# A graph layer on one core: branches taken earlier, the last four steps in another order, and DVE's picks and bf16 parts as tensor_tensor

## The reference, cut to what matters

```python
h = maximum(layernorm(x), 0)                      # x: 6250 nodes x 64
p1 = tanh(h @ pp_W1 + pp_b1) @ pp_W2 + pp_b2
inter = concatenate([p1[src], p1[dst]], -1)       # 200000 edges, dst sorted
inter = ((inter @ pi_W1 + pi_b1) @ pi_W2 + pi_b2) @ pi_W3
inter = inter.reshape(E, 64, 8)
i1 = einsum('ecb,eb->ec', inter, edge_attr)       # 8 numbers for each edge
i1 = tanh(i1 @ ii_W1 + ii_b1) @ ii_W2 + ii_b2
out = x + segment_sum(i1, dst, 6250)
```

## Time and profile before

| | |
|---|---|
| time, median of 3 runs | 2033.84 us (2032.79 to 2038.43) |
| profiled execution: its own time | 2041.94 us |
| its span | 2039.9 us |
| PE busy | 1756.2 us (86%) |
| POOL busy | 1506.6 us (74%) |
| DVE busy | 1325.6 us (65%) |
| ACT busy | 1099.3 us (54%) |
| mean granted TensorE clock | 0.939 |

### The profile page before, as it was taken

One profiled execution on the slowest core, in us unless ns is written; L12 is line 12 of the kernel. 1 busy time (PEld: TensorE's weight loads), 2 busy tenths in 40 slices (PEclk: granted clock), 3 DMA queues, 4 the chain that ended last, 5 costly groups with the idle time before them and its releaser, 6 DMA issues.

```text
span 2039.9 us, 54797 instructions
## 1 busy us (share of the span) xinstructions
PE 1756.2 (86%) x19956; PEld 1145.7 (56%) x19956; DVE 1325.6 (65%) x1894; ACT 1099.3 (54%) x2401; POOL 1506.6 (74%) x1582
## 2 busy tenths in 40 slices
PE   5698888888889888888888988989888888888988
PEld 4465555555555555555555555555555555555765
DVE  6676666666666666666666666666666666666665
ACT  4565555555555555555555555555555555555554
POOL 2777777777777777777777777777777777777774
PEclk9799999999999999999999999899999998998999
DMA  5533233222332332322323323323233233222231
GB/s 124 132 68 62 54 62 61 56 60 55 60 61 55 61 62 55 63 58 58 60 55 60 61 55 62 60 55 61 55 61 60 55 60 61 55 57 55 58 73 40
DMA packets 261682, 126.82 MB, mean 62 GB/s; under 512 B 183545, under 2 KB 233704, under 8 KB 261432
## 3 DMA queue, kind: packets, MB, share of 16 engines
q1 hardware_dynamic: 210915, 74.15, 17.1%
q0 software_dynamic: 50048, 51.35, 12.8%
q10 hardware_dynamic: 594, 0.10, 0.0%
HBM read 119.47 MB, written 6.00 MB: 62 GB/s over the span
## 4 chain that ended last, share of the span: by engine, by line
POOL 68%; issue 22%; PE 6%; DMA 2%; DVE 1%; SPq 1%; ACT 0%; DVEq 0%; ACTq 0%; POOLq 0%
POOL u_rows L453 68%; PE bank L1126 3%; PE bank L1109 1%; DMA u_rows<-u_tab,src_e 1%; PE bank L1193 1%; PE bank L1133 0%; PE spread_ps L1118 0%; DMA x_sb<-x 0%; DMA v_tab<-acc_all 0%; PE bank L1101 0%; PE spread_ps L988 0%; PE spread_ps L976 0%; ACT loc_rows L557 0%; SPq L340 0%; DMA loc_bc<-loc_tab 0%
## 5 line engine op out<-in xcount | busy, mean ns | idle before, releaser
L453 POOL DMA_INDIRECT u_rows<-u_tab,src_e x1564 | 1500.1, 959 | 509.2 <-issue 474.5
L769 DVE TENSOR_TENSOR o_sb<-st_sb,spread_ps 128x2048 f32<-128x2048 f32 x391 | 894.1, 2287 | 488.9 <-PE spread_ps L1118 485.5
L601 ACT ACTIVATE st_sb<-bank,s_bias 64x256 f32<-64x256 f32 x1564 | 734.2, 469 | 473.8 <-PE bank L1109 457.3
L1126 PE MATMUL bank<-o_sb,g_sb 128*64 128x256 f32 x6256 | 837.7, 414 | 0.8 <-ACT t_sb L592 0.8
L1126 PEld LDWEIGHTS bank<-o_sb,g_sb 128*64 128x64 f32 x6256 | 444.4, 146 | 243.7 <-issue 55.9
L1109 PE MATMUL bank<-ident,u_rows 128*128 128x128 f32 x1564 | 285.6, 306 | 231.1 <-DMA u_rows<-u_tab,src_e 230.2
L1109 PEld LDWEIGHTS bank<-ident,u_rows 128*128 128x128 f32 x1564 | 209.2, 194 | 279.4 <-DMA u_rows<-u_tab,src_e 258.7
L1193 PEld LDWEIGHTS bank<-hot,t_sb 128*65 128x65 f32 x3128 | 225.3, 144 | 158.2 <-issue 155.9
L589 ACT ACTIVATE tt_sb<-bank,z_bias 128x256 f32<-128x256 f32 x391 | 185.5, 474 | 204.5 <-PE bank L1126 204.5
L1193 PE MATMUL bank<-hot,t_sb 128*65 128x42 f32 x3128 | 272.6, 240 | 0.5 <-ACT t_sb L592 0.5
L592 ACT COPY t_sb<-bank 128x256 f32<-128x256 f32 x391 | 146.8, 376 | 221.1 <-PE bank L1133 221.1
(11 more groups left out here) (111 smaller groups left out, 223.2 us busy)
## 6 DMA issues: line engine op xcount, KB each, us to landing
loc_bc<-loc_tab SPq DMA_DIRECT2D x391, 126.0 KB
u_rows<-u_tab,src_e POOLq DMA_INDIRECT x1564
v_win<-v_tab SPq DMA_DIRECT2D x391, 15.8 KB
basis<-edge_attr SPq DMA_DIRECT2D x24, 256.0 KB, 4.0
v_tab<-acc_all SPq DMA_DIRECT2D x6, 336.0 KB
u_tab<-basis SPq DMA_DIRECT2D x6, 224.0 KB
x_sb<-x SPq DMA_DIRECT2D x1, 1120.0 KB
out<-x_sb SPq DMA_DIRECT2D x1, 784.0 KB
```

The costliest lines, as they stand in the source:

```text
L453: pool.indirect_dma_start(out=u_rows[:, g % UR, j, :], out_offset=None, in_=u_tab[:, :], in_offset=bass.IndirectOffsetOnAxis(ap=src_e[:, g ...
L601: last = nc.scalar.activation(tiles[h * D:(h + 1) * D, j], s_ps[r][part].rearrange("p (q a e) -> p q a e", q=2, a=TILES), ACT.Identity, bi ...
L769: return nc.vector.tensor_tensor(o_sb[:, r, :, :].rearrange("p c (j e) -> p j c e", j=TILES), st_sb[:, r, :].rearrange("p (j e) -> p j e", ...
L1126: last = nc.tensor.matmul(z_ps[h * D:(h + 1) * D, 0:2 * P], g_sb[:, c, :], o_sb[:, r, c, 2 * h * P:(2 * h + 2) * P], start=(c == 0), stop= ...
```

## The change

Line numbers of the changed kernel are others; here those of before are used.

1. **Picks and parts.** `pick_t` compares the places with the partition's number by `tensor_tensor` with a broadcast second input, where it was `tensor_scalar`. The two casts to bf16 are additions of a broadcast zero by `tensor_tensor`.
2. **Branches.** SP loads the flag and branches before it stores v, not behind it; the stores are in a function `store_v` that both branches call. POOL waits for u's stores inside the branch. The closing of all engines stands inside the branches, and ACT issues the 13-partition half of the last stores.
3. **v's parts** each have their own place (`v_part`), so no chunk waits for an older one's store; loc_tab is stored between v's third and fourth chunk.
4. **The last four steps** (n >= 387) on PE take the placing of the newest group last, and ACT copies s behind tanh and the copy of t in them.
5. **At the start** SP issues the eight small weight loads ahead of dst's, basis ahead of src, and PE runs 10, 3 and 4 matmuls of the identity with itself (`warm`), whose result nobody reads.

```diff
+        TURN = NG - 4
-        v_parts = acc_all[0:NP, PAIRS * NP:PAIRS * NP + VPR * 12 * D].bitcast(bf16).rearrange(
-            "p (r i w d) -> p r i w d", r=VPR, w=3, d=D)
+        def v_part(c):
+            start = PAIRS * NP + 12 * D * c if c < 4 else 12 * D * (c - 4)
+            return acc_all[0:NP, start:start + 3 * D * CHUNKS[c][1]].bitcast(bf16).rearrange(
+                "p (i w d) -> p i w d", w=3, d=D)
...
@@ SP @@
+            def store_v():
+                for c in range(NC):
+                    if c == 3:
+                        sp.wait_ge(loc_made, 1)
...
+                    sp.wait_ge(v_ready, c + 1)
...
             is_fast = sp.value_load(fast[0:1, 0:1], min_val=0, max_val=1)
             with sp.If(is_fast):
+                store_v()
...
+                store_rest()
@@ POOL @@
-            pool.wait_ge(u_stored, 32 * NC)
             with pool.If(is_fast):
+                pool.wait_ge(u_stored, 32 * NC)
                 for g in range(NG):
...
@@ ACT @@
             def v_one(c):
-                if c >= VPR:
-                    act.wait_ge(v_stored[c % VPR], 32 * (c // VPR))
...
                 for n in STEPS:
+                    if has(n) and n < TURN:
+                        make_s(n)
                     if has(n - 2):
+                        make_t(n - 2)
+                    if has(n) and n >= TURN:
+                        make_s(n)
+                store_rest()
@@ DVE @@
+            def rounded(to, of, n):
+                zero = zero1[:, 0:1].unsqueeze(2).unsqueeze(3).to_broadcast([P, n, TILES, NB])
+                return nc.vector.tensor_tensor(to, of, zero, ALU.add)
...
-                nc.vector.tensor_copy(parts_of(k)[:, :, :, 0:NB], basis_of(k)).then_inc(part1, 1)
+                rounded(parts_of(k)[:, :, :, 0:NB], basis_of(k), span_of(k)).then_inc(part1, 1)
...
-                nc.vector.tensor_copy(parts_of(k)[:, :, :, NB:2 * NB], rest_of(k)).then_inc(part2, 1)
+                rounded(parts_of(k)[:, :, :, NB:2 * NB], rest_of(k), span_of(k)).then_inc(part2, 1)
...
-                nc.vector.tensor_scalar(hot_t[:, g % 2, :], loc_bc[0:3 * W, g % VR, :], iota_p[0:3 * W, 0:1], None,
-                                        ALU.is_equal).then_inc(hot_t_ready, 1)
+                nc.vector.tensor_tensor(hot_t[:, g % 2, :], loc_bc[0:3 * W, g % VR, :],
+                                        iota_p[0:3 * W, 0:1].to_broadcast([3 * W, GE]), ALU.is_equal
+                                        ).then_inc(hot_t_ready, 1)
...
-                dve.wait_ge(acc_done, NG)
-                dve.drain().then_inc(acc_ready, 1)
+                add_late()
@@ PE @@
+            def warm(n):
+                for _ in range(n):
+                    nc.tensor.matmul(bank[7][:, 0:P], ident[:], ident[:], start=True, stop=True)
...
+                turned_step = last_pass and n + u >= TURN
+                if of(0) and not turned_step:
+                    newest()
                 if of(1):
...
                     t_transposes(u % 2).then_inc(t_ps_ready, 1)
+                if of(0) and turned_step:
+                    newest()
```

More of the change, by code:

```diff
@@ L274, in has, with store_late @@
             return 0 <= g < NG
+        def store_late(eng, b, some):
+            cols = slice(b * LPP // 2 * D, (b + 1) * LPP // 2 * D)
+            ol = out[EARLY:N, :].rearrange("(p i) d -> p (i d)", i=LPP)
+            eng.dma_start(ol[some, cols], x_sb[some, EPP * D:][:, cols]).then_inc(stored, 16)
         @block.sync
@@ L303, in load_last @@
                     "(p j) b -> p (j b)", j=TILES)).then_inc(last_in, 16)
+            col = lambda v: v.rearrange("(p a) -> p a", a=1)
+            row = lambda v: v.rearrange("(a d) -> a d", a=1)
+            twice = lambda v: v.rearrange("(a p c) -> a p c", a=1, c=1).to_broadcast([2, D, 1])
+            for dest, source in [
+                (b2col[:], col(pp_b2)), (pb1col[:], col(pi_b1)), (b2row[:], row(pi_b2)), (w3[:], pi_W3),
+                (iw1[:], ii_W1), (w_out[0:D, :], ii_W2), (w_out[D:D + 1, :], row(ii_b2)), (z_bias[:], twice(ii_b1)),
+            ]:
+                sp.dma_start(dest, source).then_inc(weights_in, 16)
             sp.wait_ge(padded, 1)
@@ L841, in add_early, with add_late @@
                                         ).then_inc(y_ready, 1)
+            def add_late():
+                for b in range(2):
+                    cols = slice((EPP + b * LPP // 2) * D, (EPP + (b + 1) * LPP // 2) * D)
+                    dve.wait_ge(y_ps, BATCHES + b + 1)
+                    nc.vector.tensor_tensor(x_sb[:, cols], x_sb[:, cols], bank[b][0:NP, 0:LPP // 2 * D], ALU.add
+                                            ).then_inc(y_ready, 1)
             with dve.If(is_fast):
@@ L954, in _ @@
                     add_early(b)
-            for b in range(2):
-                cols = slice((EPP + b * LPP // 2) * D, (EPP + (b + 1) * LPP // 2) * D)
-                dve.wait_ge(y_ps, BATCHES + b + 1)
-                nc.vector.tensor_tensor(x_sb[:, cols], x_sb[:, cols], bank[b][0:NP, 0:LPP // 2 * D], ALU.add
-                                        ).then_inc(y_ready, 1)
+                add_late()
         @block.tensor
@@ L1023, in _ @@
             last.then_inc(wprep_pe, 1)
+            warm(3)
             pe.wait_ge(wprep_act, 2)
@@ L1028, in _ @@
             last.then_inc(wprep_pe, 1)
+            warm(4)
             transposes(0)
@@ L1150, in y_early, with y_late @@
                         last.then_inc(y_ps, 1)
+            def y_late():
+                for b in range(2):
+                    for i in range(LPP // 2):
+                        last = y_slice(bank[b][0:NP, i * D:(i + 1) * D], late[:, b * LPP // 2 + i, :])
+                    last.then_inc(y_ps, 1)
             def step(n, u, first, last_pass):
@@ L1234, in _ @@
                         y_early(b, r)
-            pe.wait_ge(acc_ready, 1)
-            for b in range(2):
-                for i in range(LPP // 2):
-                    last = y_slice(bank[b][0:NP, i * D:(i + 1) * D], late[:, b * LPP // 2 + i, :])
-                last.then_inc(y_ps, 1)
+                y_late()
 NAMES = ["x", "src", "dst", "edge_attr_8"] + ["L0_gnn_" + n for n in (
```

109 lines of the change are left out of this document (51 added, 58 removed).

## The result

Device time of the changed kernel: 2094.01 us, the median of four runs (2091.78 to 2098.68), against 2036.13 us for the kernel before in its four (2032.79 to 2042.46). The ratio is 1.028, with a 95% interval of 1.0266 to 1.0297: slower. 2077 was predicted, with a range of 2036 to 2110.

What follows compares the result with a forecast made beforehand. POOL's back-to-back gathers were taken as the bound. Profiled 2041.94 us + 50 (held gathers) - 1.1 (start) - 5.6 (end) = 2085.2, or +43.3; on the median 2033.84 that gives 2077 us, range 2036 to 2110.

Steps and rivals of the forecast that it cites:

- What bounds the kernel: Whole run: POOL's back-to-back gathers bound it, 1.264 us each; PE's 4.1 us a group and DVE's added 0.32 us stay hidden.
- Contention, +50: POOL's gathers: longer tensor_tensor picks and parts on DVE hold more of them, adding 50 us.
- until that instruction ends: POOL's gather: one starting beside a running DVE instruction waits for that instruction's end; a 0.68 us one costs 0.133 us on average.
- +20 and +85: Bounds of the gather term: half the picks meet gather starts evenly, or picks tend to fall on a start.
- The rule of the start: POOL's gather: only a DVE instruction running as the gather starts holds it.
- the branch that the prediction took: Skill's rule: the gather reads its indices from SBUF, so DVE instructions with two SBUF inputs hold it; otherwise 7.4 and 1.8 us gained.
- Start, -1.1: Before the first gather: POOL's branch ahead of its wait gains 0.8 us, a warm PE 0.3; bounds 0 to -2.
- The 0.3 for a warm PE: Layer 1 at the start: warm-up matmuls speed PE's matmul pairs, gaining 0.3 us through u's chain.
- End, -5.6: Behind the last placing: reordered last steps -4.0, closing inside the branch -1.2, ACT sharing last stores -0.4 us; -3 to -6.2.
- B: Gather's start: the new instructions leave POOL alone, so the kernel is faster at 2018 us; chance 0.12.
- C: DVE and POOL slip past each other: picks fall mostly between gather starts, +10 instead of +50, 2037 us; chance 0.06.
- D: DVE and POOL lock: half of the groups held by 0.5 us, up to 2120 us; chance 0.07.

Runs made afterwards that it cites:

- run 1: Changed kernel with both picks (tensor_scalar) and parts (casts) put back as before: 2033.0 us, ratio 0.9969 to the kernel before.
- run 2: Changed kernel with only the picks put back as tensor_scalar; the parts stay tensor_tensor: 2034.3 us, ratio 0.9974 to the kernel before.
- run 3: Changed kernel with only the parts put back as casts; the picks stay tensor_tensor: 2094.1 us, ratio 1.0285 to the kernel before.
- fourth run: Kernel before with only picks and parts by tensor_tensor, nothing else of the change: 2105.1 us, ratio 1.0321.
- run 5: Changed kernel with the tensor_tensor pick's second input in PSUM instead of SBUF: 2028.3 us, ratio 0.9948 to the kernel before.
- run 6: Changed kernel with picks and parts undone, and the tensor_scalar pick run twice in a row: 2028.5 us, ratio 0.9948 to the kernel before.
- run 7: Changed kernel with parts by casts, second inputs of tensor_tensor pick and hot in PSUM, hot ahead of the pick: 2018.9 us, ratio 0.9903.
- run 8: Changed kernel with picks and parts undone, and without the 17 warm-up matmuls: 2031.3 us, ratio 0.9969 to the kernel before.
- run 9: Changed kernel with the pick's tensor_tensor cut into two halves of 256 columns: 2610.0 us, ratio 1.0266 to the kernel before.
- run 10: Changed kernel with picks and parts undone and no turned last steps: 2541.7 us, ratio 1.0001 to the kernel before.
- run 11: Kernel before with only tensor_tensor picks and the second inputs of pick and hot in PSUM: 2582.1 us, ratio 1.0163.
- twelfth run: Changed kernel with casts, hot's second input in PSUM ahead of the pick, and tensor_scalar picks reading their scalar from PSUM: 2553.2 us, ratio 1.0041.

## Why the prediction was right

**What bounds the kernel.** Right: POOL has 69% of the chain, and PE's 4.1 us and DVE's added time are hidden in the 5.2 us that a group takes. It holds for the changed kernel and runs 1 to 8; in 9 to 12 PE bounds.

**Contention, +50.** The mechanism was right, and runs 5 and 7 show it. In the two profiles POOL's busy time grows by 56.0. The long gathers account for 59.6 (20.6 to 80.2 us above the undisturbed ones), and 3.6 go back because the undisturbed gather happens to be 2 ns shorter in the profile after. Of the 59.6 the parts have 1 to 3 by runs 1 to 3, less than the 4.9 set for them, and the picks some 57, where the prediction had 52.0 - 7.4 = 44.6.

The step that was too small is "until that instruction ends". With a pick of 0.68 us between the parts' instructions and hot, holds run on through up to three instructions (1.41 us at 193.15), which the sum did not have: some 22 us. Against that, the price for a single instruction was too high: the waits for the end of the one that ran at the start are some 58 us, where the sum has 71.3. That these two nearly cancel, and that +50 stands so near to +56, is partly luck; the range's two bounds, +20 and +85, are wide enough for either. The rule of the start has a gap too, the cast that begins some 0.5 us behind it (run 7), but that is worth next to nothing. A tensor_scalar pick of 0.35 us, two in each group, leaves 12.3 us of excess in all, no more than the 0.019 us set for it gives.

**Which rule of the Trainium skill decides.** The prediction set a rule against the trace: by "Who interferes with whom" (the Trainium skill, SBUF — State Buffer), with the gather taken as one that only writes, the edit would be a gain. Run 5 agrees with the branch that the prediction took: a Vector instruction with two SBUF inputs holds a GpSimd gather that reads its indices, and with one input in PSUM it does not (excess 8.1 against 75.0). The same section counts tensor_scalar and casts among what can enter a 2-port mode and then shuts GpSimd out; the short holds beside a tensor_scalar in run 6 fit that, but no run shows which mode it ran in. So do the holds by a cast at a second moment, where no tensor_tensor was seen to hold. By its wording an instruction holds for its own whole length; the holds of 1.41 us through three instructions are longer than that, and there the measurement decides.

**Start, -1.1.** The first gather came 0.68 us earlier. The branch ahead of the wait gave less than the 0.8 taken. From the last of SP's issues of u to the first gather (rows in order of time of the fourth run and of the changed kernel):

```profile
32.73 5.50 SPq L332 DMA_DIRECT2D u_tab<-basis  x9
40.47 1.11 POOL L453 DMA_INDIRECT u_rows<-u_tab,src_e  x1 [32.81 <-DMA u_tab<-basis]
```

```profile
33.04 4.72 SPq L342 DMA_DIRECT2D u_tab<-basis  x9
```

it is 40.47 - 38.23 = 2.24 us with the old branch and 39.54 - 37.76 = 1.78 with the new one: 0.46 us. The 0.3 for a warm PE is wrong: the pairs took 2.04 us all the same. The first gather lies between 38.2 and 39.7 us in the kernels of the first two sets that share this start, so the 0.2 that is left of the 0.68 is within their scatter.

**End, -5.6.** Right: 8.4 us from placing to last sums as worked out, no gap in the closing matmuls, and 23.9 - 18.8 = 5.1 us less behind the last gather's start.

**The sum.** In the profiled runs it was 2085.2 against 2091.8 measured, 6 of contention and 0.9 of start and end. The median came out 17 us above the forecast: these 6.6, and 10.3 from the step from profile to median, since the one profile of before lay 8.1 us above the median then known and the one after lies 2.2 below its own. Between the medians the change is +57.9, where +43.3 was forecast. The range of 2036 to 2110 holds it with room. Rivals: B needed a mean gather below 959 ns, C little more than that; it is 995. D needed over 1.02 us.

## What to carry to other kernels

When one engine issues gathers back to back and is the bound, ask of every other engine's instruction not how long it is but what it does to a gather that starts beside it. Here, moving one broadcast constant to PSUM took 66 us off the changed kernel, with no instruction shorter, and left it 9 us below the kernel before. Where a pick or compare must read two tensors, try the constant in PSUM. It makes the DVE instruction no shorter, so it pays only while the gathers are the bound: the kernel before with these two edits lost 41 us (run 11) at a time when PE was the bound. And measure small differences of a sum over 1564 gathers against the undisturbed gather of the same profile: 3 ns of it are 4.7 us.

## What was not expected of the hardware

- Holds pass from one tensor_tensor to the next when they stand back to back (1.41 us through three), while between two tensor_scalars the gather mostly gets in (0.11 us). A tensor_scalar whose *scalar* lies in PSUM still holds it (21 of 41 in the twelfth run, up to 0.12 us), a tensor_tensor with either 512 or 168 elements from PSUM never did (130 and 38 in the seventh).
- A cast holds a gather at a second moment, when it begins 0.42 to 0.59 us behind the gather's start (38 of 49).
- Stream transposes and copies out of PSUM held no gather either: 33 and 2 in the changed kernel, none long.
- 17 warm-up matmuls ahead of 14 us left the pairs of layer 1 at 2.04 us. The granted clock fell to 0.50 to 0.67 between 8 and 24 us in eight of the ten kernels that had them and in none of the four without; the one pair that differs in them alone (runs 1 and 8) does not show it.
- One chip took 2039 us for the kernel before, and 2541 us about 25 minutes later, at mean granted clocks of 0.94 and 0.87. What follows PE's instructions then starts up to 2 us late, and why stays open.
